# Mixture-of-experts stage: first expert's first half in two pieces, second pair of experts chosen in the loop, last W2 tiles spread, last adds awaited by SyncE

## The reference

```python
scores = (x_flat @ Wg.T).T                        # 8 experts x 8192 tokens
top_vals, token_idx = jax.lax.top_k(scores, capacity)   # capacity 1024
token_w = jax.nn.softmax(top_vals, axis=-1)
xg = x_flat[token_idx]
h = jax.nn.silu(jnp.einsum('eic,ehc->eih', xg, W1)) * jnp.einsum('eic,ehc->eih', xg, W3)
y = jnp.einsum('eih,ech->eic', h, W2) * token_w[..., None]
out = jnp.zeros_like(x_flat).at[token_idx.reshape(-1)].add(y.reshape(-1, c))
```

## Time and profile before

| | |
|---|---|
| median of 3 runs | 828.48 us (827.77 to 828.51) |
| the profiled execution, its own time | 828.76 us |
| its span | 827.0 us |
| mean granted TensorE clock | 0.956 of full speed |
| PE busy | 757.6 us, 92% of the span |
| DVE busy | 565.8 us, 68% |
| ACT busy | 513.6 us, 62% |
| POOL busy | 367.3 us, 44% |
| share of the span in the chain that ended last: PE / DVE / POOL / DMA | 34% / 5% / 1% / 1% |

### The profile page before, as it was taken

The page is one execution under the profiler, slowest core; times in us unless marked ns, Lnnn a source line. Parts: engine busy times, 40 slices in busy tenths (PEclk is TensorE's granted clock), DMA queues, the critical chain, the costliest instruction groups (busy, mean ns, idle before and its releaser), DMA issues. The chain is left out here.

```text
span 827.0 us, 24864 instructions
## 1 busy us (share of the span) xinstructions
PE 757.6 (92%) x9590; PEld 632.6 (76%) x9590; DVE 565.8 (68%) x1449; ACT 513.6 (62%) x1001; POOL 367.3 (44%) x761
## 2 busy tenths in 40 slices
PE   6899999999999999999998613899999999999993
PEld 3788888888888888888887401688989888888983
DVE  7477787778777887788768798574654847465340
ACT  4266777776777778777767674546555555655541
POOL 6133534453435434543412321447456384746605
PEclk9799999999999999999999855899999999999997
DMA  5443435543454445434332270435536364524404
GB/s 192 141 135 119 132 96 171 171 159 119 145 179 153 133 130 196 163 121 123 123 107 82 85 225 13 142 111 95 110 73 125 90 114 122 83 37 77 46 8 51
DMA packets 76772, 97.06 MB, mean 117 GB/s; under 512 B 8264, under 2 KB 55880, under 8 KB 76616
## 3 DMA queue, kind: packets, MB, share of 16 engines
q1 hardware_dynamic: 63120, 77.52, 28.7%
q0 software_dynamic: 12288, 17.05, 12.7%
q10 hardware_dynamic: 1248, 0.92, 0.3%
HBM read 52.37 MB, written 25.72 MB: 94 GB/s over the span
## 5 line engine op out<-in xcount | busy, mean ns | idle before, releaser
L746 DVE TENSOR_REDUCE m_sb<-a_ps 128x4 f32<-128x512 f32 x256 | 164.3, 684 | 53.6 <-PE a_ps L1047 52.0
L569 ACT ACTIVATE p_t<-b_ps 128x512 f32<-128x512 f32 x252 | 141.7, 589 | 66.1 <-PE b_ps L1055 63.7
L1047 PE MATMUL a_ps<-k_st,q_st 31*128 31x128 f32 x2048 | 150.7, 285 | 5.6 <-ACT p_t L569 2.2
L1047 PEld LDWEIGHTS a_ps<-k_st,q_st 31*128 31x128 f32 x2048 | 126.7, 188 | 31.1 <-issue 24.1
L1452 POOL DMA_INDIRECT out<-y,idx_add x64 | 100.3, 1567 | 110.7 <-ACT y L1511 88.9
L1055 PE MATMUL b_ps<-q_st,k_st 32*128 32x128 f32 x1984 | 143.8, 283 | 0.0
L482 POOL TENSOR_TENSOR x<-o_n,x_res 128x256 f32<-128x256 f32 x63 | 46.1, 732 | 187.7 <-DVE o_n L836 168.8
L1055 PEld LDWEIGHTS b_ps<-q_st,k_st 32*128 32x128 f32 x1984 | 120.2, 186 | 0.0
L1698 DVE TENSOR_TENSOR act_h<-act_h,bank 128x512 f32<-128x512 f32 x64 | 44.0, 688 | 84.2 <-PE bank L1833 81.5
L1833 PE MATMUL bank<-x_hi,w_hi 128*128 128x512 f32 x254 | 100.1, 394 | 0.0
L1833 PE MATMUL bank<-x_lo,w_hi 128*128 128x512 f32 x254 | 99.0, 390 | 0.0
(11 more groups left out here) (294 smaller groups left out, 1734.3 us busy)
## 6 DMA issues: line engine op xcount, KB each, us to landing
w<-in_w_t SPq DMA_DIRECT2D x24, 512.0 KB, 5.0
rows_scratch<-xg SPq DMA_DIRECT2D x16, 528.0 KB, 4.0
x_in<-in_x SPq DMA_DIRECT2D x16, 512.0 KB, 4.7
c_t<-in_ctx_t SPq DMA_DIRECT2D x16, 512.0 KB, 4.6
k_st<-k_val SPq DMA_DIRECT2D x64, 128.0 KB
q_st<-q_val SPq DMA_DIRECT2D x64, 128.0 KB, 2.4
x_res<-in_x SPq DMA_DIRECT2D x16, 512.0 KB, 3.8
out<-x SPq DMA_DIRECT2D x16, 512.0 KB, 3.2
```

Source lines behind the costliest of these rows:

```text
L569: act.activation(p_t[b.s % 2][:, 4 * r:4 * r + 4, :], ps[q % 2][:].rearrange("p (h s) -> p h s", s=P), ACT.Exp, scale=SCALE).then_inc(exp_ ...
L746: dve.tensor_reduce(m_sb[b.s % 2][:, 4 * q:4 * q + 4], a_ps[q % 2][:].rearrange("p (h s) -> p h s", s=P), AX_X, ALU.max).then_inc(max_done, 1)
L1047: mm = pe.matmul(a_ps[i][:, t * P:(t + 1) * P], q_st[p][r:r + A_K, t, tok], k_st[p][r:r + A_K, t, tok], start=True, stop=True)
```

## The change

Expert 0's first half of 512 tokens is handled as two pieces of 256 (HALF). The first index list is made after two positions (first_list), and its gathers count on two semaphores of their own (s_first). A step of transposes, copy and subtraction now takes one piece with both column halves. On TensorE a new function, first_hidden, does for each piece the four transposes and then hidden tiles 0 and 1 (W1 and W3) at 256 columns each; only the second piece signals that a tile is done. hidden(0, 0) and hidden(0, 1) go out of the loop.

Pair 1 is chosen in the loop of expert 0 (PAIR_OF gets 0: 1). rank_tied(1), choose(1) and place_slots(1) leave VectorE's prelude and left(1) and starts(1) leave TensorE's. Six picks of expert 1 instead of four come ahead of the loop, and tokens_lo(0, 0) and (0, 1) have three positions each behind them. The split of W2 moves behind the first gate. TensorE's fillers are four, then six picks, then six.

In the last expert W2 tiles 0 and 1 go ahead of hidden tiles 6 and 7 (EARLY_AT), with their copies on ScalarE after n = 6 and n = 7. The eight waits on the last adds go from the end of GpSimd's program to the end of SyncE's.

The diff, cut where it only repeats indices and banks:

```diff
 TRANS_AT = {0: 0, 2: 1, 3: 2, 5: 3}
 SPLIT_AT = {1: 0, 3: 1, 5: 2}
 PICK_RING = 4
+EARLY_AT = {6: 0, 7: 1}
 FIND_CONSTS = 29
 LEFT_AT, START_AT, DIFF_AT, Z_AT = 0, 1, P, 511
-PAIR_OF = {1: 2, 3: 3}
+PAIR_OF = {0: 1, 1: 2, 3: 3}
...
+    HALF = SPAN // 2
...
-    mat_ps = [banks[7], banks[0], t_ps[1], t_ps[1]]
+    mat_ps = [banks[7], t_ps[1], t_ps[1], t_ps[1]]
...
-        if n < ST + TT:
+        if n < ST:
             return banks[3 + n % PICK_RING][:, 0:P + 1]
-        i = n % ST if n >= 2 * ST else n - ST - TT
-        b = later_ps[i // 3] if n >= 2 * ST else y_ps[i // 3]
+        i = n % ST
+        b = y_ps[i // 3 % 2] if n < 2 * ST else later_ps[i // 3]
         return b[:, (i % 3) * (P + 1):(i % 3 + 1) * (P + 1)]
...
+    def gathered(eng, e, h):
+
+        if e // 2 + h == 0 and e % 2 == 0:
+            for q in range(2):
+                eng.wait_ge(s_first[q], 16 * TT // 2)
+        else:
+            eng.wait_ge(s_xg[e % 2][h], 16 * TT * (e // 2 + (0 if e % 2 + h == 0 else 1)))
...
             load(e + 2)
         for p in range(2):
             sp.wait_ge(s_w[p], 48 * E // 2)
+        for st in range(ST):
+            sp.wait_ge(s_add[st], 16 * E)
...
             for h in halves:
-                pool.wait_ge(s_idx, HT * e + h + 1)
                 for st in range(h * TT, (h + 1) * TT):
+                    pool.wait_ge(s_idx, 1 if e + st // 2 == 0 else HT * e + h + 2)
+                    ready = s_first[st // 2] if e + h == 0 else s_xg[e % 2][h]
                     pool.indirect_dma_start(xg[e % 2][:, st, :], None, rows[:, :],
-                                            bass.IndirectOffsetOnAxis(ap=idx[e % 2][:, st:st + 1], axis=0)).then_inc(s_xg[e % 2][h], 16)
+                                            bass.IndirectOffsetOnAxis(ap=idx[e % 2][:, st:st + 1], axis=0)).then_inc(ready, 16)
...
         for e in range(E):
             add(e)
             gather(e + 2, range(HT))
-        for st in range(ST):
-            pool.wait_ge(s_add[st], 16 * E)
...
+                if e + h == 0:
+                    act.activation(x_hi[0][:, :, i * HALF:(i + 1) * HALF], t_ps[i][:].rearrange("p (k n) -> p k n", k=KD),
+                                   ACT.Copy).then_inc(x_hi_done, 1)
+                else:
+                    act.activation(x_hi[e % 2][:, k, h * SPAN:(h + 1) * SPAN], t_ps[i % 2][:, 0:SPAN], ACT.Copy).then_inc(x_hi_done, 1)
...
+                if e == E - 1 and n in EARLY_AT:
+                    y_copy(e, EARLY_AT[n])
             product_hi(e, HID - 1)
-            for st in range(ST):
+            for st in range(len(EARLY_AT) if e == E - 1 else 0, ST):
                 y_copy(e, st)
...
             if e < E:
                 for st in sts:
                     n = ST * e + st
-                    dve.wait_ge(s_pick, n + 1 if n < ST + TT else ST * e + sts[-1] + 1)
+                    dve.wait_ge(s_pick, n + 1 if n < ST else ST * e + sts[-1] + 1)
...
+        def first_list(q):
+            cols = slice(q * TT // 2, (q + 1) * TT // 2)
+            dve.wait_ge(s_pos, (q + 1) * TT // 2)
+            dve.tensor_copy(idx[0][:, cols], pos[:, cols]).then_inc(s_idx, 1)
...
@@ -1707,19 +1736,18 @@
         rank_tied(0)
         choose(0)
         place_slots(0)
-        for h in range(HT):
-            positions(0, range(h * TT, (h + 1) * TT))
-            list_of(0, h)
+        for q in range(2):
+            positions(0, range(q * TT // 2, (q + 1) * TT // 2))
+            first_list(q)
+        positions(0, range(TT, ST))
+        list_of(0, 1)
         weights_lo(0, 0)
         weights_lo(0, 1)
-        rank_tied(1)
-        choose(1)
-        place_slots(1)
-        positions(1, range(0, TT))
+        tokens_lo(0, 0)
+        positions(1, range(0, 3))
+        tokens_lo(0, 1)
+        positions(1, range(3, 6))
         list_of(1, 0)
-        tokens_lo(0, 0)
-        tokens_lo(0, 1)
-        weights_lo(0, 2)
...
                 if n > 0:
                     product_lo(e, n - 1)
+                if (e, n) == (0, 0):
+                    weights_lo(0, 2)
                 if e == 0 and n == 1:
-                    positions(1, range(TT, TT + 3))
-                if e == 0 and n == 2:
-                    positions(1, range(TT + 3, ST))
+                    positions(1, range(6, ST))
                     list_of(1, 1)
...
-            if a > 1:
-                pe.wait_ge(t_out, TRANS * (2 * a - 2))
+            if a > 0:
+                pe.wait_ge(t_out, TRANS * max(2 * a - 2, 1))
...
-                    if n < ST + TT:
+                    if n < ST:
                         wait(pe, s_pos, n - (PICK_RING - 1))
+                    if e == 1 and st > 5:
+                        pe.wait_ge(s_pos, ST + 3)
...
+                if e + h == 0:
+                    pe.wait_ge(s_first[i], 16 * TT // 2)
+                    for c in range(KD):
+                        for t in range(TT // 2):
+                            at = c * HALF + t * P
+                            mm = pe.transpose(t_ps[i][:, at:at + P], xg[0][:, i * (TT // 2) + t, c * P:(c + 1) * P], ident[:])
+                    mm.then_inc(t_done, 1)
+                    return
+                gathered(pe, e, h)
...
+        def first_products(ps, i, n, q):
+
+            f, cols = slice(n * P, (n + 1) * P), slice(q * HALF, (q + 1) * HALF)
+            passes_ = [(w_, x_, k) for w_, x_ in ((w_hi, x_hi), (w_lo, x_hi), (w_hi, x_lo)) for k in range(KD)]
+            for m, (w_, x_, k) in enumerate(passes_):
+                if x_ is x_lo:
+                    pe.wait_ge(t_out, q + 1)
+                mm = pe.matmul(ps[n][:, cols], w_[0][i][:, k, f], x_[0][:, k, cols], start=(m == 0), stop=(m == len(passes_) - 1))
             return mm
+
+        def first_hidden():
+
+            pe.wait_ge(w_lo_done, 2)
+            pe.wait_ge(s_pos, ST)
+            for q in range(2):
+                transposes(0, q)
+                pe.wait_ge(x_hi_done, q + 1)
+                for n in range(2):
+                    for i, ps, done in ((0, h1_ps, h1_done), (1, h3_ps, h3_done)):
+                        mm = first_products(ps, i, n, q)
+                        if q == 1:
+                            mm.then_inc(done, 1)
 
         def hidden(e, n):
             h, f = n // FT, slice((n % FT) * P, (n % FT + 1) * P)
             if n == 0:
                 pe.wait_ge(w_lo_done, 3 * e + 2)
-                pe.wait_ge(s_pos, ST + TT if e == 0 else min(ST * (e + 2), ST * E))
-            if e + n == 0:
-                first_products(f).then_inc(h1_done, 1)
+                pe.wait_ge(s_pos, min(ST * (e + 2), ST * E))
             if n % FT == 0:
                 pe.wait_ge(t_out, TRANS * e + KD * (h + 1))
             wait(pe, silu_done, HID * e + n - 1)
-            if e + n > 0:
-                products(h1_ps[n % 2], e, 0, f, h).then_inc(h1_done, 1)
+            products(h1_ps[n % 2], e, 0, f, h).then_inc(h1_done, 1)
             wait(pe, gate_done, HID * e + n - 1)
             products(h3_ps[n % 2], e, 1, f, h).then_inc(h3_done, 1)
...
         left(0)
         starts(0)
         picks(0, range(ST))
+        busy(t_ps[1], 4)
+        pe.wait_ge(s_pos, ST)
+        picks(1, range(0, 6))
         busy(t_ps[1], 6)
-        left(1)
-        busy(t_ps[1], 2)
-        starts(1)
-        picks(1, range(0, TT))
-        pe.wait_ge(s_begun, 4)
-        transposes(0, 0)
-        transposes(0, 1)
-        pe.wait_ge(s_pos, ST + TT)
-        busy(y_ps[1], 2)
+        first_hidden()
...
                 if (e, n) == (0, 2):
                     transposes(0, 2)
                     transposes(0, 3)
-                hidden(e, n)
-                if e == 0 and n == 0:
-                    picks(1, range(TT, TT + 3))
+                if e > 0 or n > 1:
+                    hidden(e, n)
                 if e == 0 and n == 1:
-                    picks(1, range(TT + 3, ST))
+                    picks(1, range(6, ST))
                 if n == (3 if e == 0 else 1):
                     if e == 0:
                         pe.wait_ge(s_pos, 2 * ST)
@@ -1912,8 +1953,11 @@
                     left(a)
                 if a is not None and n == HID - 1:
                     starts(a)
+                if e == E - 1 and n + 1 in EARLY_AT:
+                    down(e, EARLY_AT[n + 1])
             for st in range(ST):
-                down(e, st)
+                if e < E - 1 or st >= len(EARLY_AT):
+                    down(e, st)
```

More of the change, by code:

```diff
@@ L1651, in list_of @@
                 for i in range(HT):
-                    wait(dve, s_xg[e % 2][i], 16 * TT * (e // 2))
+                    if e > 1:
+                        gathered(dve, e - 2, i)
                 dve.wait_ge(s_pos, ST * e + (h + 1) * TT)
@@ L1682, in raw @@
                 for h in range(HT):
-                    dve.wait_ge(s_xg[e % 2][h], 16 * TT * (e // 2 + 1))
+                    gathered(dve, e, h)
                 wait(dve, s_es, e)
@@ L1835, in products @@
             return mm
-        def first_products(f):
```

(13 more changed lines are left out.)

12 lines of the change are left out of this document (8 added, 4 removed).

## The result

The changed kernel took 823.08 us (median of 6 runs, 822.28 to 825.47), the kernel before 827.58 beside it (6 runs, 826.83 to 828.51): ratio 0.9947, 95% interval 0.9938 to 0.9957, 4.5 us less. Its profiled execution took 823.12 with a span of 821.4 (before 828.76 and 827.0). The forecast was 824.0. On another chip the same kernel gave only 0.9974 (experiment after_again); what that does to each step is the second half of this document.

What follows compares the result with a forecast made beforehand. TensorE was taken to bound the kernel almost without a break, leaving gains only at head and tail: -1.3 - 0.9 - 2.3 = -4.5 on 828.76 gives 824.3, or 824.0 for the median; range 822.2 to 827.0 us.

Steps and rivals of the forecast that it cites:

- Head, first piece: Start of expert 0: transposes of the first 256 tokens at 516.8, their products from 518.55.
- two bounds: Start of the first transposes: gather allows 516.5, 2.89 us after its issue; TensorE's fillers and picks end about 516.8.
- Rival 2: TensorE's clock is high through both pieces of expert 0: 822.7 us, chance 0.15.
- Until the fifth tile: Expert 0: the fifth hidden tile starts 3.3 us earlier, at 534.3, with the third SiLU late next.
- The stand: TensorE waits 1.8 us for VectorE's diff ahead of expert 2's picks; 2.0 us cost with 0.2 for starts.
- Rival 4: No TensorE wait at expert 2's picks, because VectorE is further ahead than its order says: 822.0 us, chance 0.06.
- the head's net: Head of the layer: 3.3 us gained until the fifth hidden tile, 2.0 lost at expert 2's picks, together -1.3 us.
- Tiles spread: Last expert: two W2 tiles between the last hidden tiles make GpSimd's last add start 0.9 us earlier.
- Waits on SyncE: Kernel end: GpSimd's DRAIN takes its 4.31 us beside the last add's flight, 2.3 us gained.
- Rival 1: Kernel end: GpSimd's DRAIN waits for the last add's landing, so moving the waits gains nothing: 826.3 us, chance 0.20.
- The 12 ns: Trainium skill's DRAIN figure of about 12 ns, against 4307 ns traced; by it moving the waits would gain nothing.
- Rival 5: TensorE's clock falls for 6.8 us after each of three gaps at the head: slower, 833.4 us, chance 0.04.

Runs made afterwards that it cites:

- after_again: The changed kernel with no edit, run once more on a third chip: 826.48 us, 0.9974 of the kernel before.
- place_sooner: The changed kernel with the second pair's choosing in expert 0 one hidden tile earlier, begun and diff ahead of the last gate: 820.94 us, 0.9914.
- head_alone: The changed kernel with both tail parts undone, so only the change at the head of the layer is left: 828.56 us, 0.9998.
- early_alone: The kernel before with only W2 tiles 0 and 1 of the last expert ahead of hidden tiles 6 and 7: 826.78 us, 0.9985.
- sp_alone: The kernel before with only the eight waits on the last adds moved from GpSimd to SyncE: 825.53 us, 0.9968.

## Why the prediction was right, and where it was lucky

The sum of -4.5 was measured as -4.5 on the chip where the change was timed. By its steps:

- **Head, first piece.** Transposes began at 517.18 (forecast 516.8) and products at 518.49 (518.55), in a trace that starts the stage 0.32 sooner. The forecast start rested on two bounds, and both were off. The gather takes 3.91 us from its issue to the transposes (place_sooner) and not 2.89, as its issue alone took 1.94 (the last section has the row). The fillers ended at 517.12 (515.63 + 1.49), later than I took, and just covered it. The piece was not one third at the low clock: 3.39 us at 1.00, with 2.8 forecast for that clock. Rival 2, the clock high through both pieces, held in that execution, and the gap of 1.12 was 0.2 smaller than the 1.35.
- **Until the fifth tile.** 3.65 us gained against 3.3 forecast. As predicted, the third SiLU is what is late next (wait of 0.4 at line 1871), and the three small matmuls hide in that wait.
- **The stand.** 1.88 us against 1.8, released by diff. Rival 4 (no stand) is wrong. I had the clock's fall behind it only as an upper bound. head_alone shows it: 3.4 us at 0.50, or 1.7 us, and four of the five profiles with this stand have such a fall. This is the term that was most likely mis-sized: the head's net was to be -1.3, and measured by itself it is -0.2 us (-1.0 to +0.6) by the times and -0.6 (-1.3 to 0.0) by the spans. That interval reaches to the forecast, so how much was missed is not shown.
- **Tiles spread.** 1.2 us by early_alone, and 1.3 by the last add's start against the last copy's (4.38 and 3.08), against 0.9. I let the third add start 0.79 behind its copy; it started 0.36 behind (805.98, and the copy ends at 805.14 + 0.48). GpSimd never went idle from the second add on, so there was no such start, and seven adds follow from 804.12 instead of six from 808.25.
- **Waits on SyncE.** 2.5 us in the profile and 2.6 (1.7 to 3.6) by sp_alone, against 2.3. Rival 1 is wrong: the DRAIN runs beside the landing. In the trace it ends 4.3 us behind GpSimd's last issue, much like the 4.31 of rows 4.
- **The 12 ns.** The 12 ns that the Trainium skill gives (VectorE: DVE Perf Modes, The DRAIN you can't avoid) do not hold for GpSimd at this kernel's end: with them there would have been nothing to hide behind the landing, and 2.6 us came.

So the right total came partly by luck, from a head forecast about 1.1 too good by the times (-1.3 for -0.2; 0.7 by the spans) and a tail forecast about 0.7 too small (-3.2 for -3.9). Rival 5, the clock falling after the gaps, named the right mechanism with the wrong size: it took 6.8 us at each of three gaps, and the traces show some 3.4 us, at the stand in four of five profiles, and behind the lengthened gap of the pieces in one of four. On after_again's chip the change is worth 2.1 us and not 4.5, which the range (to 827.0) holds, but for a reason that none of its cases names.

The version that beats both kernels is place_sooner (0.9914); with the transposes moved as well it kept 0.9912 and 0.9926 on the later ones, where the change alone had 0.9974.

## What to carry to other kernels

When work ahead of a loop is moved into it, price the first consumer that now stands, and then what a standing TensorE does to its own clock. Hide a copy that feeds TensorE by putting its transposes one tile ahead, even where the trace shows the gap as free: it is cover against a late start. Time the changed kernel itself in every batch of experiments, on the same chip: with a reference from the chip of the result the kernels of the later chips read 2.2 us worse than with after_again's, and as that one too is another chip's, neither reading is sure.

## What the runs showed of the hardware that I had not expected

- The same kernel on two chips differed by 3.4 us (823.08 and 826.48), while the kernel before differed by 1.0 or less (827.58 to 828.59); the ratios differ by 0.0027, or 2.2 us. ScalarE's copy started 1.70 us behind the end of a group of transposes on one and 0.04 on the other.
- A stand of 1.9 us, with TensorE busy for 1.52 of 3.40 us, was followed by 3.4 us at half clock in head_alone and by none in the changed kernel's first profile.
- GpSimd's DRAIN at the end took 4.3 us beyond its last issue and ran beside the transfer in flight.
- The second gather took 1.94 us to issue (1.06 before), and no row shows why. It cost nothing in the changed kernel's first profile, as TensorE's fillers ended behind its landing; in after_again, place_sooner and head_alone TensorE waited 1.00, 0.20 and 1.07 us for the gather ahead of the transposes:

```profile
513.30 1.94 POOL L1457 DMA_INDIRECT xg<-rows_scratch,idx  x1 [0.30 <-DVE idx L1674]
```
